# Weights and first context of the wide attentions split one stage earlier, relu attention's keys and values made two batches ahead, last stores awaited by the gathers

## The reference, cut to what matters

```python
# layer 1 ("relu attention")
qp = relu(q @ Wq + bias_q); kp = relu(k @ Wk + bias_k); vp = relu(v @ Wv + bias_v)
scores = relu(einsum('bqe,bke->bqk', qp, kp))
out = relu(einsum('bqk,bke->bqe', scores / sqrt(256) + mask, vp))
# layers 2 and 3 ("wide attentions"; layer 3 with biases)
qh, kh, vh = (q @ Wq), (k @ Wk), (v @ Wv)        # 256 -> 1024, 16 heads of 64
attn = softmax(einsum('bhqd,bhkd->bhqk', qh, kh) / 8)
out = einsum('bhqk,bhkd->bhqd', attn, vh) @ Wo
...
x = x + L1_xattn(layernorm(x), ctx, ctx, mask, ...)
x = x + L1_ffn(layernorm(x), ...)
x = x + L2_xattn(layernorm(x), ctx, ctx, ...)
x = x + L2_ffn(layernorm(x), ...)
x = x + L3_xattn(layernorm(x), ctx, ctx, ...)
```

## Time and profile before

| | us |
|---|---|
| runs | 3428.69, 3431.1, 3436.66 (median 3431.1) |
| profiled execution | 3437.43 |
| its span, first to last instruction | 3435.6 |
| mean granted TensorE clock | 0.948 |
| L0t's last store issued to L1x's first matmul | 784.47 to 786.76 |
| L1t's last store issued to L2's first matmul | 1432.90 to 1444.01 |
| L2t's last y taken to L3's first key taken | 2385.51 to 2398.44 |

### The profile page before, as it was taken

One profiled execution on the slowest core, in us unless ns is written; L12 is line 12 of the kernel. 1 busy time (PEld: TensorE's weight loads), 2 busy tenths in 40 slices (PEclk: granted clock), 3 DMA queues, 4 the chain that ended last, 5 costly groups with the idle time before them and its releaser, 6 DMA issues. The chain is left out here.

```text
span 3435.6 us, 60328 instructions
## 1 busy us (share of the span) xinstructions
PE 3106.0 (90%) x21966; PEld 2609.6 (76%) x21966; DVE 1658.8 (48%) x3470; ACT 1563.6 (46%) x4177; POOL 1319.2 (38%) x1417
## 2 busy tenths in 40 slices
PE   5888858998989869899999999598999999997999
PEld 4776748996756559778888887488788888876998
DVE  4777760003566557544444444301444444445766
ACT  2554523443345435445555555244555555552232
POOL 0000001112100022167777777211577777773433
PEclk8999969999999869999999999699999999996999
DMA  5555535552100044200000000464000000001332
GB/s 143 135 132 128 131 134 198 183 183 74 50 1 1 4 165 141 66 20 15 12 14 14 15 13 1 168 217 138 13 13 12 12 13 13 12 1 53 114 106 89
DMA packets 146134, 253.21 MB, mean 74 GB/s; under 512 B 46892, under 2 KB 122664, under 8 KB 133304
## 3 DMA queue, kind: packets, MB, share of 16 engines
q1 hardware_dynamic: 132216, 223.67, 21.7%
q0 software_dynamic: 8064, 20.20, 2.1%
q10 hardware_dynamic: 5568, 5.51, 0.5%
HBM read 214.85 MB, written 34.46 MB: 73 GB/s over the span
## 5 line engine op out<-in xcount | busy, mean ns | idle before, releaser
L719 POOL TENSOR_SCALAR L_probs<-L_probs,L_inverse 112x375 f32<-112x375 f32 x512 | 653.0, 1275 | 119.3 <-issue 119.3
L867 DVE TENSOR_REDUCE L_negmax<-bank 112x1 f32<-112x375 f32 x768 | 394.7, 542 | 428.1 <-PE bank L471 356.3
L675 ACT ACTIVATE L_probs<-bank,L_negmax 112x375 f32<-112x375 f32 x768 | 435.2, 572 | 216.7 <-DVE L_negmax L867 211.9
L498 PE MATMUL bank<-ident,L_probs 112*125 112x112 f32 x2304 | 399.4, 282 | 19.2 <-POOL L_probs L719 12.9
L498 PEld LDWEIGHTS bank<-ident,L_probs 112*125 112x125 f32 x2304 | 338.0, 189 | 91.1 <-issue 49.6
L717 POOL TENSOR_TENSOR L_inverse<-L_sums,neg_one 112x1 f32<-112x1 f32 x512 | 297.2, 580 | 141.4 <-ACT L_probs L675 141.1
L655 ACT ACTIVATE L_probsT<-bank 125x336 f32<-125x336 f32 x512 | 231.9, 453 | 248.4 <-PE bank L498 248.3
L637 ACT ACTIVATE v<-bank 125x512 f32<-125x512 f32 x192 | 114.8, 598 | 266.6 <-PE bank L424 266.6
L705 POOL TENSOR_TENSOR L_stats<-L_stats,neg_half 112x1 f32<-112x1 f32 x48 | 27.0, 563 | 520.6 <-DVE L_stats L784 520.6
L513 PE MATMUL bank<-L_probsT,v 125*64 125x112 f32 x3072 | 206.7, 270 | 1.8 <-ACT L_probsT L655 1.1
L417 PE MATMUL bank<-L_ctx_hi,L_wk_hi 128*128 128x376 f32 x512 | 149.5, 373 | 30.2 <-DVE L_ctx_lo L851 22.7
(11 more groups left out here) (327 smaller groups left out, 7109.2 us busy)
## 6 DMA issues: line engine op xcount, KB each, us to landing
L0t_w<-in_F_w SPq DMA_DIRECT2D x35, 1024.0 KB, 4.9
L_keys<-spread_k SPq DMA_DIRECT2D x64, 376.0 KB, 6.7
L2t_w<-in_F_w SPq DMA_DIRECT2D x21, 1024.0 KB, 4.9
L_ctxT<-in_ctxT SPq DMA_DIRECT2D x48, 375.0 KB, 3.1
w_all<-in_F_w SPq DMA_DIRECT2D x16, 1024.0 KB
cap_w<-in_F_w SPq DMA_DIRECT2D x16, 1024.0 KB, 5.2
L3d_row<-comb_rows SPq DMA_DIRECT2D x64, 224.0 KB, 3.2
L_q<-spread_q SPq DMA_DIRECT2D x128, 56.0 KB, 2.2
```

The costliest lines, as they stand in the source:

```text
L498: ins = pe.transpose(psT[h % len(psT)][0:SJ, j * T:(j + 1) * T], probs[h % NB][:, j * SJ:(j + 1) * SJ], core.ident[0:T, 0:T])
L675: act.activation(probs[e % NB][:, :], psS[e % 2][0:T, 0:S], ACT.Exp, bias=negmax[b.par][:, e:e + 1], accum_out=sums[b.par][:, e:e + 1]).th ...
L719: pool.tensor_scalar(probs[h % NB][:, :], probs[h % NB][:, :], inverse[b.par][:, h:h + 1], None, ALU.mult)\
L867: dve.tensor_reduce(negmax[b.par][:, h:h + 1], psS[h % 2][0:T, 0:S], AX, ALU.max, negate=True).then_inc(maxed.sem, 1)
```

## The change

Three things.

1. **The wide attentions' splits move one stage ahead.** `wk_hi`, `wk_lo`, `wv_hi`, `wv_lo` and the first context with its split parts are held tensors. `wide_loads` has a fifth load, of context 0. In L1t ACT and DVE make the splits after the last expert's hidden parts, before `take_y` and `take_out`; the expert's own split weights and one of the two `ys` share this memory. In L2t DVE does both halves of the splits in quarters at tiles 12 to 15 and the context's at tile 16. `cross_attention` does none of it and its first load is that of context 1.
2. **Relu attention** makes keys and values two batches ahead. `first` also makes keys and values of batch 1, most of it before the transposes of batch 0, and in the loop Y of b comes before the query product of b+1 and the values of b+2. `add_experts` moves behind the mixing of b, also two ahead.
3. **The last stores.** SP no longer waits for them at the end of L0t and L2t, and in L1t only for the even buffer. POOL waits for both counters ahead of the first gather of the next attention; ACT waits for both ahead of V0, since V0's memory may be the store's source.

```diff
+            for s in slots_stored:
+                pool.wait_ge(s.sem, s.at(0))
             for n in range(4):
                 gather(n)
...
-        load_wide(Batch(0, 0))
         next_ctx(Batch(0, 1))
...
-        act.wait_ge(wide_weights.sem, wide_weights.at(64))
-        for whole, high in ((wk, wk_hi), (wv, wv_hi)):
-            act.activation(high[:, :, :], whole, ACT.Copy).then_inc(w_high.sem, 1)
...
+def split_first_ctx(core, dve):
+    whole, high, low = (core.held["wide_ctx" + n] for n in ("", "_hi", "_lo"))
+    here, split = core.counter("ctx_here0"), core.counter("ctx_split")
+    dve.memset(whole[:, :, S:SP], 0.0)
+    dve.wait_ge(here.sem, here.at(16))
+    dve.drain()
+    dve.tensor_copy(high[:, :, :], whole[:, :, :])
+    dve.drain()
+    dve.tensor_tensor(low[:, :, :], whole[:, :, :], high[:, :, :].bitcast(F32), ALU.subtract).then_inc(split.sem, 1)
...
-                for i in range(2):
-                    sp.wait_ge(stored[i].sem, stored[i].at(16 * ((NT + 1 - i) // 2)))
...
                 for t in range(NT):
+                    if split_ahead and 12 <= t < 16:
+                        split_wide((t - 12) // DC, (t - 12) % DC)
+                    if split_ahead and t == 16:
+                        split_first_ctx(core, dve)
...
+                act.wait_ge(wide_weights.sem, wide_weights.at(64))
+                act.activation(w1_hi[:, :, :], core.held["v0"][:, 0:DC, :], ACT.Copy).then_inc(w1_high.sem, 1)
+                act.wait_ge(y_made.sem, y_made.at(NT - 1))
+                act.activation(core.held["wv_hi"][:, :, :], core.held["v1"][:, 0:DC, :], ACT.Copy).then_inc(w1_high.sem, 1)
                 take_out(NT - 1)
...
+                def split_wide():
+                    for n, c in enumerate("kv"):
+                        dve.wait_ge(w1_high.sem, w1_high.at(NT + n + 1))
+                        low, high = core.held[f"w{c}_lo"], core.held[f"w{c}_hi"]
+                        dve.tensor_tensor(low[:, :, :], core.held[f"v{n}"][:, 0:DC, :], high[:, :, :].bitcast(F32),
+                                          ALU.subtract).then_inc(w1_split.sem, 1)
+                        if n == 0:
+                            split_first_ctx(core, dve)
...
                 def first(b):
                     keys(b)
-                    queries(b)
                     for j in range(J):
                         values(b, j)
+                    keys(b + 1)
+                    values(b + 1, 0)
+                    queries(b)
+                    values(b + 1, 1)
+                    values(b + 1, 2)
                     queries_end(b)
...
                     ins.then_inc(scored.sem, 1)
+                    if more:
+                        keys(b + 2)
                     if not last:
-                        keys(b + 1)
                         queries(b + 1)
-                        values(b + 1, 0)
-                        queries_end(b + 1)
-                        values(b + 1, 1)
-                        values(b + 1, 2)
...
                     ins.then_inc(made["Y"].sem, 1)
+                    if not last:
+                        queries_end(b + 1)
+                    if more:
+                        for j in range(J):
+                            values(b + 2, j)
...
     def wide_loads(w):
         return [(h["v0"][:, 0:DC, :], w["wk"], sem("wide_weights")), (h["v1"][:, 0:DC, :], w["wv"], sem("wide_weights")),
-                (h["wq"][:, :, :], w["wq"], sem("wide_weights")), (h["wo"][:, :, :], w["wo"], sem("wide_weights"))]
+                (h["wq"][:, :, :], w["wq"], sem("wide_weights")), (h["wo"][:, :, :], w["wo"], sem("wide_weights")),
+                (h["wide_ctx"][:, :, 0:S], a["ctxT"][0], sem("ctx_here0"))]
```

More of the change, by code:

```diff
@@ L233, in cross_attention @@
         if wide:
-            w_high = core.counter("w_high")
-        if wide:
+            slots_stored = [core.counter(f"y_stored{i}") for i in range(2)]
             wide_weights = core.counter("wide_weights")
@@ L685, in first @@
                             act.wait_ge(weights.sem, weights.at(16 * nweights))
+                        if wide and p == "V0":
+                            for s in slots_stored:
+                                act.wait_ge(s.sem, s.at(0))
                         take(p, b, where[p][0])
@@ L1500, in resident_tiles @@
         hidden = sb("hidden", [P, F, tile])
-        ys = [sb(f"ys{i}", [tile, D]) for i in range(2)]
+        ys = [core.held[f"ys{i}"] for i in range(2)]
         rows_here = [core.counter(f"rows_here{i}") for i in range(2)]
@@ L2464, in gather @@
                             .then_inc(gathered[n % 4].sem, 16)
+                for i in range(2):
+                    s = core.counter(f"y_stored{i}")
+                    pool.wait_ge(s.sem, s.at(0))
                 for n in range(4):
@@ L2579, in first, with heads @@
                 def first(b):
-                    take(b)
+                    take_keys(b)
                     for j in range(J):
                         take_values(b, j)
+                    take_keys(b + 1)
+                    take_tokens(b)
+                    for j in range(J):
+                        take_values(b + 1, j)
                     take_queries(b)
-                def heads(b, last):
+                def heads(b, last, more):
+                    if more:
+                        take_keys(b + 2)
                     if not last:
-                        take(b + 1)
-                        take_values(b + 1, 0)
+                        take_tokens(b + 1)
                         take_queries(b + 1)
-                        take_values(b + 1, 1)
-                        take_values(b + 1, 2)
+                    if more:
+                        for j in range(J):
+                            take_values(b + 2, j)
                 run(act, first, heads)
@@ L2625, in first @@
                 def first(b):
+                    for j in range(J):
+                        bias_values(b, j)
                     add_experts(b.n)
@@ L2629, in first, with heads @@
                     for j in range(J):
-                        bias_values(b, j)
-                def heads(b, last):
-                    if not last:
-                        add_experts(b.n + 1)
-                        normalise_start(dve, stats, batch_row(core.x, b + 1), var_ready)
+                        bias_values(b + 1, j)
+                    add_experts(b.n + 1)
+                    normalise_start(dve, stats, batch_row(core.x, b + 1), var_ready)
+                def heads(b, last, more):
                     dve.wait_ge(scored.sem, scored.at(b.n + 1))
@@ L2644, in heads @@
                         .then_inc(mixed.sem, 1)
-                    if not last:
-                        for j in range(J):
-                            bias_values(b + 1, j)
+                    if more:
+                        add_experts(b.n + 2)
+                        normalise_start(dve, stats, batch_row(core.x, b + 2), var_ready)
                     dve.wait_ge(made["Y"].sem, made["Y"].at(b.n + 1))
@@ L2652, in heads @@
                         .then_inc(taken["Y"].sem, 1)
+                    if more:
+                        for j in range(J):
+                            bias_values(b + 2, j)
                 run(dve, first, heads)
@@ L3198, in STAGES @@
     wide = {"wq": [P, DC, E], "wo": [P, E // P, D], "v0": [P, J, E], "v1": [P, J, E]}
+    ahead = {"wide_ctx": [P, DC, SP], "wide_ctx_hi": [P, DC, SP], "wide_ctx_lo": [P, DC, SP]}
+    for n in ("wk_hi", "wk_lo", "wv_hi", "wv_lo"):
+        ahead[n] = [P, DC, E]
+    tile_out = {f"ys{i}": [TILE, D] for i in range(2)}
     of_relu = {"relu_wq": [P, DC, D], "relu_wk": [P, DC, D], "relu_wv": [P, DC, D], "relu_bq": [P, DC],
```

83 lines of the change are left out of this document (45 added, 38 removed).

## The result

The change made the kernel faster: 3413.99 us median against 3429.24, a ratio of 0.9955 with a 95% interval of 0.9942 to 0.9968, so 11 to 20 us (13 runs of each, median difference 15.3). The forecast had been 21.7 us.

What follows compares the result with a forecast made beforehand. TensorE, busy 90% of the span, bounds the kernel, so only its waits at stage borders can be won. 6.5 + 11.1 + 5.4 - 1.3 = 21.7 us, from the median 3431.1 to 3409.4 us; range 3401 to 3420.

Steps and rivals of the forecast that it cites:

- L1x: Relu attention: scores 3.9 us sooner, last two passes save 5.15, less 2.2 uncovered work and 0.3 clock: 6.5 us gained.
- L1t's splits: End of L1t: ACT's and DVE's splits end 0.6 us before DVE must take y, so they cost nothing.
- L2: Wide attention: first matmul at 1433.8 for 1444.01, 10.2 us, plus 0.9 from fuller clock: 11.1 us gained.
- L2t: Expert stage: fifth load stands ahead of tile 3's weights, 1.0 us transfer plus 0.35 issue: 1.3 us lost.
- L3: Wide attention: K0 taken 6.2 us sooner, when the biases land, less 0.8 for the clock: 5.4 us gained.
- Stage starts: Barriers after L0t, L1t and L2t: without SP's store wait, the next stages start 1.5, 3.0 and 1.4 us earlier.
- The second rival: Stage barriers: the store's wait was not what held them; 5.9 us less gain, 3415 us; chance 0.06.
- the clock had hardly fallen, and I charge 0.3: L1x's start: PE idles 3.5 us ahead of the transposes, with the clock hardly falling; 0.3 us charged.
- After a gap under 2 us I expect full clock mostly: L2's start: first key pieces run mostly at full clock, gaining 0.9 of 1.2 us.
- the first rival: L2 and L3: another wait takes the place, halving their gains; gain 13.4 us, time 3418; chance 0.12.
- the smaller charge from the rows: L3, ahead of K2: slow clock loses 1.3 us, 0.5 won back, 0.8 charged; the skill's pricing nearly 2.
- The loop rival: L1x's loop: passes get slower as Y waits behind `add_experts`; at 2.2 us a pass 31 us lost; chance 0.03.

Runs made afterwards that it cites:

- e3: The changed kernel with SyncE waiting for the last stores again in L0t, L1t and L2t; 3416.94 us, ratio 0.9956 to the kernel before.
- e1: The kernel before with only the relu attention's new order, without its wait for the stores; 3428.60 us against 3432.86, ratio 0.9986.
- e4: The changed kernel with the old relu order and SyncE waiting for the stores, leaving the splits alone; 3422.42 us, ratio 0.9964 to before.
- e9: The changed kernel with L3's biases loaded in L2t, two gathers before the root, and SyncE waiting for stores in L0t alone; 3408.46 us, ratio 0.9925 to before.
- e8: The changed kernel timed a second time, unmodified, against the kernel before; 3406.98 us, ratio 0.9931.
- e11: The changed kernel timed a third time, unmodified, against the kernel before; 3411.00 us, ratio 0.9942.
- e5: The changed kernel with L3's four bias tensors loaded in L2t at tile 6; 3407.25 us against before's 3431.21, ratio 0.9930.
- e6: The changed kernel with only two batches' gathers ahead of the first root in L1x, L2 and L3; 3406.22 us, ratio 0.9924 to before.
- e10: The changed kernel with both the early biases of e5 and the two gathers first of e6, timed again; 3402.29 us, ratio 0.9915 to before.
- e2: The changed kernel with the old order in relu attention, POOL still awaiting the stores; 3414.64 us, ratio 0.9948 to before.
- e7: The changed kernel with the edits of e5 and e6 together, first timing; 3404.99 us, ratio 0.9921 to before.

## Why the prediction was right, and where it was off

The time and its cause were right: the change is faster by three gains at three starts. The median of the first comparison, 3413.99, lies in the range 3401 to 3420; its gain, 15.3 us, is at the low end of the forecast's 15.2 to 25.8, the later two, 24.2 and 21.2, are well inside. Term by term, gains in us from the table, for the three profiles of the change:

| term | forecast | measured |
|---|---|---|
| L1x | 6.5 | 5.3, 4.8, 6.8 |
| L1t's splits | 0 | -0.5, -0.9, -0.7 |
| L2 | 11.1 | 7.1, 9.1, 9.1 |
| L2t | -1.3 | -0.2, -1.4, -1.1 |
| L3 | 5.4 | 6.2, 5.6, 6.0 |
| sum | 21.7 | 17.9, 17.2, 20.1 |

The sums' mean, 18.4, lies near the mean of the three timed gains (15.3, 24.2, 21.2: 20.2).

- **Stage starts: right, their worth too high.** 1.5, 3.0 and 1.4 us were forecast, e3 gave 1.4, 2.9 and 1.4. The second rival (the store's wait did not hold the barrier) is out. But the forecast let the sum, 5.9 us, reach the end, and by e3's stages about 2 us of it did, within the scatter of single executions.
- **L1x: the sum nearly right, two of its terms off against each other.** The step that failed is "the clock had hardly fallen, and I charge 0.3". It rested on one row, 2.76 us for the keys after 2.97 us of idling. The same idle of 2.96 to 2.99 us ahead of the same keys gave 4.45 (e1), 5.34 (e3), 4.36 (e4) and 4.39 us (e9): the row of before was the exception. In e8 the gap ahead of the transposes cost 1.74 + 0.84 = 2.6 us at half clock, in e11 1.5. That eats what the earlier start brought: after the last y the scores come 2.4, 1.3 and 2.4 us sooner in the three profiles of the change, for the forecast's 3.9, and e1, which starts later, has them 3.2 us sooner. On the other side, the loop did not keep 8.93 us but takes 8.81, 1.7 us in 14 passes, which I had not seen.
- **L2: the first matmul right, the rest too high.** 10.1 us were gained at the first matmul (12.1 us after L1t's last transposes, then 2.0), against 10.2. "After a gap under 2 us I expect full clock mostly" failed in all three profiles of the change: the window of 1428.4 has clock 0.57, and PE had already waited 1.37 us ahead of L1t's last transposes, which I had not counted. V0 came 10.4 to 10.7 us sooner there; in e5 and e6, where the first keys ran at full clock, 11.9. What was lost later is a wait in two of three profiles (1.42 and 1.34 us at V2, the first rival's kind: another wait takes the place), and a longer wait in the first batch, with a fall of the clock behind it:

```profile
1484.42 1.24 POOL L718 TENSOR_SCALAR L_probs<-L_probs,L_inverse 112x375 f32<-112x375 f32 x1 [3.59 <-issue]
...
1485.72 0.58 PE L496 MATMUL bank<-ident,L_probs 112*125 112x112 f32 x3 [2.50 <-POOL L_probs L718]
```

  This wait on POOL, behind two gathers, exists in before too (1.74 us); in the change it was 2.31 to 2.50. How often the clock falls in L2's first 130 us is a part of its length: not once in e5 (770.2 us), twice in e9, for 13.7 us in all (776.8). Another part lies at L2's end. e6 and e10, with the same start and one fall each, differ by 2.9 us, and their last 25 us of attention differ in the clock (e6's window first):

```profile
2131.90:2157.00 25.10, 17.57 (x121) 14.16 (x117) 5.53 (x16) 6.66 (x17) 11.61 (x13) 0.73 0.01 1
```

```profile
2122.80:2147.90 25.10, 21.69 (x125) 17.57 (x125) 3.57 (x8) 5.82 (x16) 11.92 (x13) 0.52 0.00 1
```

  From the first product with Wo of the last batch but one to the last of all, e6 takes 32.3 us and e10 34.6. The batches before that follow each other at 43.8 to 44.1 us in every kernel here, before included.
- **L3: right, 0.5 us too low, with two terms off against each other.** K0 was taken with the last bias's landing; PE idled 3.53 us ahead of K2 for the 4.6 forecast, and the clock fell (0.55). The Trainium skill (TensorE: Matmul & The Clock Gate, Terms) prices throttled time at its length times (1 - K/N), by which, as the forecast estimated, L3 would have won 4.5; the stages give 5.6 to 6.2, so the smaller charge from the rows was the nearer one. e3 and e4, in which SyncE waits, win 5.5 and 5.4 us: of the 1.4 us of the earlier start only some 0.5 reached L3's end, and the splits were worth more than the 4.0 that the forecast leaves them.
- **L2t: right on average**, 0.9 for 1.3, with tile 3's wait at 4.76, 5.06 (e8) and 5.30 (e11) for the 5.5 to 6 forecast, 4.41 before.
- **L1t: the cover held** (DVE waited 0.75 us for PE; the forecast's own terms make its 0.6 us of slack 0.8), yet the stage is 0.5 to 0.9 us longer than before, in which e1's 172.1 shows 0.3 of plain scatter. What makes the rest was not tried.
- **The loop rival** (a slower pass) is out: PE is busy 45.00 of 45.

## What to carry to other kernels

An engine that starts earlier must have its whole work earlier: look which input comes last, and whether it sits behind queued work (here a root behind eight gathers) that a later order would let pass. And of two equal idle times the one ahead of slack can be the cheaper, since the slow clock that follows is paid where the work hangs: e3's scores came no later than the change's, though it started 1.4 us later. Starts moved by 5.6 us in all were worth some 2 us at the end here. Price the clock after a gap from several rows, never from one.

## What the runs showed of the hardware that was not expected

- Equal gaps do not give equal clocks. After 2.96 to 2.99 us of idling the same eight key matmuls took 2.76 us once and 4.36 to 5.34 us four times. At L2's start nine profiles (the change, e2 and e5 to e11) have the same two gaps, 1.37 us ahead of L1t's last transposes and 1.73 ahead of the keys: in five (the change, e2, e7, e8, e11) the first keys ran at half clock, in four (e5, e6, e9, e10) at full clock, and V0 came 1.3 to 1.6 us sooner.
- The dense experts have two paces at the same granted clock. In windows of 200 us of before and of the change PE was busy throughout:

```profile
3185.90:3385.90 200.00, 200.00 (x970) 181.63 (x969) 134.40 (x158) 60.42 (x112) 80.91 (x54) 1.00 0.36 111
```

```profile
3166.60:3366.60 200.00, 200.00 (x988) 185.33 (x987) 143.58 (x160) 61.58 (x114) 80.22 (x56) 1.00 0.37 112
```

  970 matmuls in one, 988 in the other. Five of the 13 profiles have the slower pace (dense 312.5 to 313.6 us), the change in e8 among them, one lies between (308.7), and seven have 307.4 to 307.7, so it is not the change's doing. What sets it stays open. It is 5 us of each comparison's scatter.
